# Folding the head weights with 128-row products, moving the output's fold beside the mixes, and running five stages as one block in a fp32 transformer kernel

## The reference

```python
x = x + attn_a(layernorm(x), q_a_w, q_b_w, kv_a_w, kv_b_w, o_w)   # 16 heads
x = x + ffn(layernorm(x), Wg, Wu, Wd, Wr, temperature)            # 8 experts
x = x + attn_b(layernorm(x), wq, wk, wv, wo)                      # 16 causal heads
x = x + ffn(layernorm(x), Wg, Wu, Wd, Wr, temperature)
# attn_a: low-rank queries and keys, the parts that matter here
q   = x @ q_a_w.T @ q_b_w.T          # rank 192, then 16 heads of 64 (pass) + 64 (rotated)
ckv = x @ kv_a_w.T                   # 64 compressed + 64 shared rotated
kvb = ckv[..., :64] @ kv_b_w.T       # per head: 64 of the key (pass), 128 of the value
scores = query . key;  attn = softmax(scores);  out = (attn @ v) @ o_w.T
```

## Time and profile before

| | us |
|---|---|
| median of 3 runs | 1534.94 |
| lowest, highest | 1534.45, 1535.30 |
| the profiled execution | 1532.65 |
| its span, first to last instruction | 1530.80 |

### The profile page before, as it was taken

The page is one execution under the profiler, slowest core; times in us unless marked ns, Lnnn a source line. Parts: engine busy times, 40 slices in busy tenths (PEclk is TensorE's granted clock), DMA queues, the critical chain, the costliest instruction groups (busy, mean ns, idle before and its releaser), DMA issues. The chain is left out here.

```text
span 1530.8 us, 26737 instructions
## 1 busy us (share of the span) xinstructions
PE 1460.8 (95%) x8904; PEld 1262.2 (82%) x8904; DVE 1171.8 (77%) x2661; ACT 835.6 (55%) x2040; POOL 612.7 (40%) x484
## 2 busy tenths in 40 slices
PE   8799999997899999988999999999999879999998
PEld 6677777776788888876899999999999868888887
DVE  7899999998765555587888888888888777555554
ACT  4788888885433333227766666666666433333322
POOL 2587777874100000017766656666666210000000
PEclk9899999999999999999999999999999999999999
DMA  2265555555210000003223223213222200010001
GB/s 101 55 162 145 148 148 149 155 129 141 84 42 21 22 21 0 1 4 98 52 70 69 63 63 69 70 43 86 67 49 52 53 22 22 21 42 21 0 0 56
DMA packets 73156, 100.17 MB, mean 65 GB/s; under 512 B 10304, under 2 KB 63552, under 8 KB 73024
## 3 DMA queue, kind: packets, MB, share of 16 engines
q1 hardware_dynamic: 73024, 98.55, 24.5%
HBM read 37.56 MB, written 2.23 MB: 26 GB/s over the span
## 5 line engine op out<-in xcount | busy, mean ns | idle before, releaser
L1840 DVE TENSOR_TENSOR f_hidden<-ps,f_silu 128x512 f32<-128x512 f32 x128 | 87.7, 690 | 201.5 <-PE ps L122 201.5
L482 POOL TENSOR_TENSOR ab_swapped<-ab_swapped,const 128x512 f32<-128x512 f32 x126 | 162.9, 1293 | 166.9 <-ACT ab_swapped L477 166.1
L1731 ACT ACTIVATE f_silu<-ps 128x512 f32<-128x512 f32 x128 | 76.3, 598 | 276.2 <-PE ps L122 276.2
L120 PE MATMUL ps<-xh,f_wl 128*128 128x512 f32 x512 | 203.2, 397 | 1.6 <-DVE f_hidden L1840 1.6
L121 PE MATMUL ps<-xl,f_wh 128*128 128x512 f32 x512 | 202.8, 396 | 0.0
L122 PE MATMUL ps<-xh,f_wh 128*128 128x512 f32 x512 | 202.5, 396 | 0.0
L1543 POOL TENSOR_TENSOR ab_qk<-ab_qk,ab_swapped 128x512 f32<-128x512 f32 x126 | 172.5, 1369 | 9.9
L1311 ACT ACTIVATE ab_probs<-ab_probs,ab_negmax 128x128 f32<-128x128 f32 (+1 forms) x256 | 114.6, 449 | 81.9 <-DVE ab_negmax L1414 77.5
L73 POOL TENSOR_TENSOR rstd<-shifted,minus_half 128x4 f32<-128x4 f32 x16 | 16.2, 1013 | 339.6 <-DVE shifted L67 339.6
L120 PE MATMUL ps<-f_wh,f_hl 128*128 128x256 f32 x512 | 144.2, 282 | 0.4 <-DVE x L1856 0.4
L121 PE MATMUL ps<-f_wl,f_hh 128*128 128x256 f32 x512 | 143.9, 281 | 0.0
(11 more groups left out here) (210 smaller groups left out, 4377.8 us busy)
## 6 DMA issues: line engine op xcount, KB each, us to landing
ab_probsT<-ab_squares SPq DMA_DIRECT2D x128, 192.0 KB, 3.6
aa_probsT<-f_stages SPq DMA_DIRECT2D x128, 128.0 KB, 2.6
b_stages<-keys SPq DMA_DIRECT2D x128, 128.0 KB, 2.8
f_stages<-wf_in SPq DMA_DIRECT2D x16, 768.0 KB, 4.4
aa_spread<-inv_rows SPq DMA_DIRECT2D x64, 128.0 KB, 3.0
b_stages<-wb_qkv_in SPq DMA_DIRECT2D x8, 768.0 KB, 6.4
a_stage<-wa_in SPq DMA_DIRECT2D x8, 608.0 KB, 4.3
x<-x_in SPq DMA_DIRECT2D x4, 512.0 KB, 7.2
```

Of the source, the lines that this page charges most:

```text
L120: nc.tensor.matmul(out, ll, rh, start=start, stop=False)
L482: return engine.tensor_tensor(by_batch(out), by_batch(src), table(c, rows, col), ALU.mult)
L1840: nc.vector.tensor_tensor(hidden[:, m, :], UP(m), silu[:, m, :], ALU.mult).then_inc(hid_done, 1)
```

## The change

1. The key weights of a pair of heads are laid out as a block diagonal of 128 rows by 128 columns (zeros off the diagonal), so `stage` grows by 64 columns. The query's fold becomes two products of 128 rows and 128 columns, without the wait between the heads; ACT's four copies become two, DVE's two subtractions one (in the opening, its four become two).
2. The output's fold moves on PE from j = 1 to j = 2, between the scores and the mixes; on ACT and DVE from j = 2 to j = 3.
3. One `nc.Block()` holds all stages, so the four barriers between them are gone. Waits are added where a barrier had ordered things: SP before it reloads stage (`first_fold_lo`), SP at the end of attention_a (`pv_done`) and of experts (`w_lo`), PE ahead of the router's products (`own_norm.lo_done`).

```diff
-A_PASS, A_K, A_ROT, A_V, A_O = 0, 256, 320, 576, 704
-A_COLS = 1216
+A_PASS, A_K, A_ROT, A_V, A_O = 0, 256, 384, 640, 768
+A_COLS = 1280
...
-def opening(nc, c, name, a, x, const, small, temperature, order, weights, stage, stage_in):
+def opening(nc, c, block, name, a, x, const, small, temperature, order, weights, stage, stage_in):
...
-                fold_product(nc, SPARE[:, 0:P], stage, 0).then_inc(fold_ready, 1)
-
-                pe.wait_ge(fold_ready, 1)
-                fold_product(nc, SPARE[:, P:2 * P], stage, 1)
+                fold_product(nc, SPARE[:, 0:2 * P], stage)
                 fold_output_product(nc, SPARE[:, 2 * P:], stage).then_inc(a.wo_ready, 1)
...
-def fold_product(nc, bank, stage, h):
-
-    r = slice(64 * h, 64 * h + 64)
+def fold_product(nc, bank, stage):
+
     for m in range(2):
-        ins = nc.tensor.matmul(bank[:, m * KVR:(m + 1) * KVR], stage[r, A_PASS + m * P:A_PASS + (m + 1) * P], stage[r, A_K:A_K + KVR], start=True, stop=True)
+        ins = nc.tensor.matmul(bank[:, m * P:(m + 1) * P], stage[:, A_PASS + m * P:A_PASS + (m + 1) * P], stage[:, A_K:A_K + 2 * KVR], start=True, stop=True)
     return ins
...
+def both_heads(columns):
+
+    return columns.rearrange("p (m h d) -> p m h d", m=2, h=2)
+
+
+def fold_parts(bank, stage, w):
+
+    return ((w[:, :, :, 0:KVR], both_heads(bank[:, 0:4 * KVR])), (w[:, :, :, KVR:P], both_heads(stage[:, A_ROT:A_ROT + 4 * ROT])))
+
+
+def fold_upper(nc, bank, stage, wh):
+    for upper, source in fold_parts(bank, stage, wh):
         ins = nc.scalar.copy(upper, source)
     return ins
...
                 sp.wait_ge(wo_ready, it)
+                if it == 1:
+                    sp.wait_ge(a.first_fold_lo, 1)
                 after(sp, fold_rest, it - 1)
...
             fetch(sp, ahead)
 
+            sp.wait_ge(pv_done, 2 * SLOTS)
+
...
-                fold_product(nc, FOLD(it)[:, 0:P], stage, 0).then_inc(fold_ready, 1)
-
-                pe.wait_ge(fold_ready, 2 * it - 1)
-                fold_product(nc, FOLD(it)[:, P:2 * P], stage, 1).then_inc(fold_ready, 1)
+                fold_product(nc, FOLD(it)[:, 0:2 * P], stage).then_inc(fold_ready, 1)
...
-                if j == 1 and s == 1 and it + 1 < HP:
-
-                    pe.wait_ge(fold_lo, it + 1)
-                    pe.wait_ge(rope_read, 4)
-                    pe.wait_ge(swap_done, 4)
-                    fold_output(it + 1, FOLDS)
                 if j == 2:
+                    if s == 1 and it + 1 < HP:
+
+                        pe.wait_ge(fold_lo, it + 1)
+                        pe.wait_ge(rope_read, 4)
+                        pe.wait_ge(swap_done, 4)
+                        fold_output(it + 1, FOLDS)
                     mix(n, 0)
                     mix(n, 1)
...
-                act.wait_ge(fold_ready, 2 * it)
-                for h in range(2):
-                    ins = fold_upper(nc, FOLD(it)[:, h * P:(h + 1) * P], stage, wh[:, it % 2], h)
-                ins.then_inc(fold_hi, 1)
+                act.wait_ge(fold_ready, it)
+                fold_upper(nc, FOLD(it)[:, 0:2 * P], stage, wh[:, it % 2]).then_inc(fold_hi, 1)
...
-                if j == 2 and s == 1 and it + 1 < HP:
+                if j == 3 and s == 1 and it + 1 < HP:
                     fold_output(it + 1, FOLDS)
...
-                for h in range(2):
-                    (upper, source), _ = fold_parts(FOLD(it)[:, h * P:(h + 1) * P], stage, wh[:, it % 2], h)
-                    ins = nc.vector.tensor_tensor(wl[:, it % 2, :, h, 0:KVR], source, upper.bitcast(F32), ALU.subtract)
-                ins.then_inc(fold_lo, 1)
+                (upper, source), _ = fold_parts(FOLD(it)[:, 0:2 * P], stage, wh[:, it % 2])
+                nc.vector.tensor_tensor(wl[:, it % 2, :, :, 0:KVR], source, upper.bitcast(F32), ALU.subtract).then_inc(fold_lo, 1)
...
-                if j == 2 and s == 1 and not last:
+                if j == 3 and s == 1 and not last:
                     fold_output(it + 1, FOLDS)
...
+            sp.wait_ge(w_lo, 2 * TURNS)
             if result:
...
             def router_products():
 
+                pe.wait_ge(own_norm.lo_done, KD * (NG - 1))
...
         c.ps = ctx.enter_context(nc.psum_tensor("ps", [P, 8, 512], F32))
+        block = ctx.enter_context(nc.Block())
```

More of the change, by code:

```diff
@@ L250, in fold @@
                 act.wait_ge(a.wo_ready, 1)
-                for h in range(2):
-                    ins = fold_upper(nc, SPARE[:, h * P:(h + 1) * P], stage, a.wh[:, 0], h)
-                ins.then_inc(fold_hi, 1)
+                fold_upper(nc, SPARE[:, 0:2 * P], stage, a.wh[:, 0]).then_inc(fold_hi, 1)
                 nc.scalar.copy(a.woh[:, 0, :], SPARE[:, 2 * P:]).then_inc(a.wo_hi, 1)
@@ L422, in keys_lo_parts, with fold_lower @@
     return engine.tensor_tensor(in_fours(a.kl[:, slot]), every_fourth(a.keys[:, slot]), in_fours(a.kh[:, slot].bitcast(F32)), ALU.subtract)
-def fold_product(nc, bank, stage, h):
-    r = slice(64 * h, 64 * h + 64)
+def fold_product(nc, bank, stage):
     for m in range(2):
-        ins = nc.tensor.matmul(bank[:, m * KVR:(m + 1) * KVR], stage[r, A_PASS + m * P:A_PASS + (m + 1) * P], stage[r, A_K:A_K + KVR], start=True, stop=True)
+        ins = nc.tensor.matmul(bank[:, m * P:(m + 1) * P], stage[:, A_PASS + m * P:A_PASS + (m + 1) * P], stage[:, A_K:A_K + 2 * KVR], start=True, stop=True)
     return ins
[L433 to L440, removed]
+def both_heads(columns):
[4 more added lines that the diff above has]
+    for upper, source in fold_parts(bank, stage, wh):
         ins = nc.scalar.copy(upper, source)
     return ins
-def fold_lower(nc, bank, stage, wh, wl, h):
-    for (upper, source), (lower, _) in zip(fold_parts(bank, stage, wh, h), fold_parts(bank, stage, wl, h)):
+def fold_lower(nc, bank, stage, wh, wl):
+    for (upper, source), (lower, _) in zip(fold_parts(bank, stage, wh), fold_parts(bank, stage, wl)):
         ins = nc.vector.tensor_tensor(lower, source, upper.bitcast(F32), ALU.subtract)
@@ L513, in fold_output_product, with attention_a @@
     return ins
-def attention_a(nc, c, name, a, weights, stage, stage_in, norm, ahead):
+def attention_a(nc, c, block, name, a, weights, stage, stage_in, norm, ahead):
     SQ, LEAD, SLOTS = 32, 6, HP * NG
@@ L1056, in first_projections_b, with attention_b @@
         ins.then_inc(b.proj_ready, 1)
-def attention_b(nc, c, name, b, w_qkv, w_out, stage, wo_stage, stage_in, wo_in, own_norm, norm, ahead):
+def attention_b(nc, c, block, name, b, w_qkv, w_out, stage, wo_stage, stage_in, wo_in, own_norm, norm, ahead):
     W, SQ, LEAD = T + P, 32, 7
@@ L1108, in attention_b @@
         own_banks = [MIX(1), OUT]
-        block = ctx.enter_context(nc.Block())
         @block.sync
@@ L1548, in _, with experts @@
                 norm_rstd(nc, c, norm, pool, s)
-def experts(nc, c, name, weights, stage, stage_in, own_norm, ahead=(), norm=None, result=None, b=None):
+def experts(nc, c, block, name, weights, stage, stage_in, own_norm, ahead=(), norm=None, result=None, b=None):
     with ExitStack() as ctx:
@@ L1959, in hybrid_kernel @@
             a.swap_done, a.sin_done, a.rotated, a.q_hi, a.q_lo = sem("swap_done"), sem("sin_done"), sem("rotated"), sem("q_hi"), sem("q_lo")
+            a.first_fold_lo = sem("first_fold_lo")
             a.inv_rows = nc.dram_tensor("inv_rows", (2, 2 * TG, P), F32, kind="Internal").ap()
             a.squares, a.probsT = [f_stages[:, 0:2 * PAIRS * T], a.keys[:]], b_stages[:]
-            opening(nc, c, "open", a, x, const, small, temperature, order, wa, a_stage, a_in)
-            attention_a(nc, c, "aa", a, wa, a_stage, a_in, norm2, [(f_stage[:, e], wf[e], f1_in[e]) for e in range(2)])
+            opening(nc, c, block, "open", a, x, const, small, temperature, order, wa, a_stage, a_in)
+            attention_a(nc, c, block, "aa", a, wa, a_stage, a_in, norm2, [(f_stage[:, e], wf[e], f1_in[e]) for e in range(2)])
         with ExitStack() as inner:
@@ L1970, in hybrid_kernel @@
             b.stage, b.wo_stage, b.stage_in, b.wo_in = b_stage, bo_stage, b_in, bo_in
-            experts(nc, c, "f1", wf, f_stage, f1_in, norm2, ahead=[(b_stage[:], wb_qkv[0], b_in), (bo_stage[:], wb_out[0], bo_in)], norm=norm3, b=b)
-            attention_b(nc, c, "ab", b, wb_qkv, wb_out, b_stage, bo_stage, b_in, bo_in, norm3, norm4, [(f_stage[:, e], wf[e], f2_in[e]) for e in range(2)])
-        experts(nc, c, "f2", wf, f_stage, f2_in, norm4, result=(out.rearrange("(t p) d -> p t d", p=P), stored))
+            experts(nc, c, block, "f1", wf, f_stage, f1_in, norm2, ahead=[(b_stage[:], wb_qkv[0], b_in), (bo_stage[:], wb_out[0], bo_in)], norm=norm3, b=b)
+            attention_b(nc, c, block, "ab", b, wb_qkv, wb_out, b_stage, bo_stage, b_in, bo_in, norm3, norm4, [(f_stage[:, e], wf[e], f2_in[e]) for e in range(2)])
+        experts(nc, c, block, "f2", wf, f_stage, f2_in, norm4, result=(out.rearrange("(t p) d -> p t d", p=P), stored))
 def constants():
@@ L2025 @@
     kvb = w["L0_attn_a_kv_b_w"].reshape(HP, 2, NOPE + VD, KVR)
```

(5 more changed lines are left out.)

11 lines of the change are left out of this document (2 added, 9 removed).

## The result

| | before | after |
|---|---|---|
| median of 6 runs each, us | 1534.89 | 1525.55 |
| lowest, highest | 1530.34, 1538.15 | 1523.53, 1527.36 |
| the profiled execution | 1532.65 | 1524.99 |
| its span | 1530.80 | 1523.11 |

The ratio after to before is 0.994, with a 95% interval of 0.9924 to 0.9955: the kernel is 0.6% faster. The forecast was 1528.0, its range 1523.8 to 1532.4. One execution of a kernel further down (the one with the sine product last) took 1999 us at a granted clock of 0.66; it is left out of that kernel's numbers.

The account below looks back on a forecast made before the run. The prediction took DVE to bound attention_a. Output's fold 4.1, query's fold 1.3 and barriers 1.5 sum to 6.9 us, taking 1534.94 to 1528.0 us; range 1523.8 to 1532.4.

Parts of the forecast that it names:

- What bounds the kernel: In attention_a the chain of waits ends in DVE; its waits for ACT's folded weights, 15.8 us, are what the change can take.
- the output's fold next to the mixes: PE's four instructions in attention_a: 0.7 us standing alone, 0.4 us next to mixes using the same 64-column tiles.
- The output's fold: attention_a, slot s=1: step 2 shrinks 0.93 us, step 3 grows 0.34; net 0.58 us seven times, 4.1 us.
- The query's fold: attention_a: fewer ACT copies and DVE subtractions save 0.21 us six times, 1.3 us; PE's freed 0.9 to 1.0 worth nothing.
- The barriers: Four stage edges: 0.4 us at each expert layer and into attention_b, 0.3 into attention_a; together 1.5 us, bounds 0.5 to 3.0.
- The start of attention_a: Barrier into attention_a: DVE could start 0.8 us sooner but needs PE's scores after its warming products; gain 0.3 us.
- (1): Rival: in attention_a DVE still waits in step 3 because ACT's copy is late; sum 3.0 us, 1531.9 us; chance 12%.
- (2): Rival: PE's saved time counts in full in attention_a, 8.8 us, with barriers 10.3; 1524.6 us; chance 8%.
- (3): Rival: thinner PE work drops attention_a's clock to half, so PE bounds; a quarter at half clock gives 1548 us; chance 4%.
- a half clock between 100 and 370 us: Listed sign that the forecast is wrong: a granted clock at half in that span of the trace.
- (4): Rival: the change does not do what it says, engines merely meet elsewhere; within 1 us of 1534.9; chance 6%.
- The clock at the edges: Half-clock stretches may come or go at stage edges with the program unchanged, each worth a little over 1 us either way.

Follow-up runs that it names:

- e6: Changed kernel plus three extra identity products on PE in slots 0 and 2 of each pair of heads; 1525.88 us, ratio 0.9943, pair 39.5 us.
- e7: Changed kernel with DVE's subtraction of the query's fold moved from j=2 to j=3; 1517.80 us, ratio 0.9893, pair 38.3 us.
- e8: Changed kernel with DVE's addition to the output put ahead of its sine product in step 2; 1518.77 us, ratio 0.9907, pair 38.8 us.
- e4: Changed kernel with the query's fold as products of 64 rows again, with the wait between heads and four copies; 1527.43 us, ratio 0.9957.
- e5: Changed kernel with only PE's part of the output's fold back at j=1, ACT and DVE kept at j=3; 1525.95 us, ratio 0.9947.
- e3: Changed kernel with the output's fold back in its old place on PE, ACT and DVE; 1528.45 us, ratio 0.9961.
- e1: Kernel before with only the barriers removed (one block and its added waits), folds as before; 1531.17 us, ratio 0.9986.
- e2: Changed kernel with the four barriers back (a block for each stage), new folds kept; 1527.76 us, ratio 0.9957.
- e9: Changed kernel with both the query's subtraction one step later and the sine product after the output addition; 1509.81 us, ratio 0.9852.
- e10: Kernel of e9 plus the three extra identity products on PE in slots 0 and 2 of each pair, as in e6; 1509.95 us, ratio 0.9855.

## Why the prediction was right

**What bounds the kernel: right.** DVE's path. e6 adds 1.07 us of PE a pair and changes nothing; e7 and e8 take waits from DVE and shorten the pair by as much. PE's freed time (0.93 us in the query's fold, forecast 0.9 to 1.0) was worth nothing, as e4 and e5 show from the other side. One term on PE was too high: the output's fold next to the mixes was put at 0.4 instead of 0.7 us and takes 0.49 instead of 0.58 (start to the next product's start); it was not part of the sum.

**The output's fold: right.** Forecast 0.58 us seven times, 4.1; measured 0.60 a pair, and 4.1 us in the loop of e3. The step that mattered was that step 2 would shrink by 0.93 and not by wait plus subtraction, since the sine product moves back under POOL's addition. It did: it takes 1.12 us again and ends at 124.04, 0.55 us after POOL's 122.19 + 1.30. e8 shows that this cover was a cost in its own right.

**The query's fold: right.** Forecast 0.21 six times, 1.3; measured 4.53 to 4.31, and 1.3 us in e4. ACT's two copies took 0.71 us where 0.70 was put. One reading went further than its row: that products of 64 rows run one after the other at this place. Between the two heads stood a semaphore wait, and the products of one head use the same rows, so no run here shows what two heads' products without that wait would do. It changed nothing, since PE's part was put at nothing and e4 shows that it is.

**The barriers: inside the bounds, somewhat low.** Forecast 1.5 us; the rests of e1 and e2 differ by 2.4, inside the bounds of 0.5 to 3.0. The three edges that can be read came out at or above the forecast of 0.4 us each: 0.40 into attention_b, 0.65 to 0.94 into f1 and 0.59 into f2, 1.6 to 1.9 in place of 1.2. Part of each shows as idle time gone where the prediction had seen it: PE's turn into attention_b comes 0.42 us sooner, and the last normalised rows before each expert layer 0.47 us sooner after PE's previous turn (388.38 - 384.06 = 4.32 against 395.49 - 390.70 = 4.79; 1238.42 - 1233.44 = 4.98 against 5.45). The start of attention_a, forecast at 0.3, isn't settled. The rest of the 2.4 us lies there and in where the half-clock stretches fell.

**The sum.** Loop 5.3 us (forecast 4.1 + 1.3 = 5.4) and rest 2.4 (forecast 1.5) are 7.7, the difference of the two spans (1530.80 - 1523.11). Forecast 6.9; the 0.9 between lie in the rest, in the barriers and in the clock at the edges. The medians lie 9.3 us apart. The rest of that is scatter: the ratio's interval is 6.9 to 11.7 us.

**The rivals.** (1), DVE waiting in step 3, is refuted by the timeline (no wait before 125.27). (2) by e6. (3), a half clock in attention_a, didn't come: the granted clock of the pair is 1.00, at 94% PE, and in e9 too. Taken by the letter its sign did come, "a half clock between 100 and 370 us": one runs from 367.8 to 374.7. But the loop had ended at 359.46, and in the kernel before such a stretch followed its loop as well (375.2 to 378.6, after 365.41). (4) by e2 to e4, in which the parts come back one by one. Rival (2) would have given 1524.6, nearer to the median than the forecast: a total near a rival's number doesn't tell for it, the stages do.

**The clock at the edges.** I had allowed for one or two stretches at half clock coming or going, each worth "a little over 1 us". Over the twelve programs the time at half clock is 30.7, 34.1 or 37.6 us. The rests scatter too much to price it: without barriers they run from 1216.5 to 1217.6 us at 30.7, from 1217.7 to 1218.1 at 34.1, and are 1217.8 and 1218.8 at 37.6. The edge into f2 prices it: 12.35 us without and 13.27 with such a stretch, 0.92 us. In the kernel before a stretch lay on the first products of f1; after the change there is none at that place, and one at 1238.2 to 1241.6 us that wasn't there, at an edge where seven kernels with the same instructions have none. The Trainium skill (TensorE: Matmul & The Clock Gate, section "Part 1: The HAM clock gate") says that the gate's window runs free of the program; the rows agree with it.

## What to carry to other kernels

Find the engine whose waits end the chain, and lay its steps side by side with and without the suspected work: the difference, not the wait plus the instruction, is what a move can bring, since the next instruction may fall back under another cover. Once one move of a consumer one step behind its producer's copy has paid, look for the same pattern elsewhere (here e7, worth 7.2 us of the loop, where the whole change had brought 5.3), and for two engines that read SBUF at the same moment (e8). Check a wait's named releaser by the times and the semaphore in the code. Compare variants by the stretch that was edited, and use totals only as a check, when the clock at stage edges moves by as much as the effect.

## What the runs showed of the hardware

**DVE behind POOL.** DVE's product of two SBUF operands (64 x 512) takes 0.69 us alone. Started 0.15 us or more before the end of POOL's addition of two SBUF operands, it ended 0.55 to 0.56 us after that end in all 223 cases of the twelve traces, whether it had started 0.2 or 1.1 us ahead: from 0.73 to 1.66 us long, mostly 1.12 or 1.49. Instructions of DVE with an input in PSUM ran beside POOL in 0.65 to 0.69 us, as long as without it. The other way round stands once in each trace: POOL's subtraction took 1.60 us instead of 1.29 when it started 0.2 us into DVE's product, which kept its 0.69. The Trainium skill (SBUF — State Buffer, section "Who interferes with whom") says that a DVE instruction with two SBUF inputs contends with a GpSimd instruction that reads SBUF, and one with at most one doesn't, and that the second to start is blocked and not slowed; the traces agree with all three. I had used the 0.55 us in the forecast, but had not seen that the order of two DVE instructions gives it back: 5.1 us in the loop of e8.

**PE at 100% of a pair.** In e10 the record has PE busy for 37.10 of 37.10 us with the pair no longer than at 36.40, and with 1.07 us of products added (as e6 measured them). A full row of PE is thus not proof that PE bounds; adding products and timing the pair tells.

**A barrier between stages** cost 0.40, 0.59 and 0.65 to 0.94 us at the three edges where it can be read, of which 0.4 to 0.5 is idle time of the engine next in line. What the fourth costs is open.
